# The order of TensorE's work in the softmax layer, and the routing of tokens inside the linear layer

## The reference

```python
att = where(causal, q @ k.T * SCALE, -inf)        # 16 heads of 16, 1024 tokens a batch
y = softmax(att) @ v @ W_proj + b_proj            # softmax layer
y = x @ weight.T + pooled(x) @ disha              # its second half, one matrix here
# linear layer: Q, K = elu(x @ W) + 1;  out = num / den with running sums over tokens
num = Q @ cumsum(K.T V);  den = max(Q . cumsum(K), 1e-6);  x + (num / den) @ Wo
x + gelu(layernorm(x) @ Wf1) @ Wf2
# mixture of experts: 8 experts, 2 per token, 1.05 capacity
probs = softmax(xf @ Wg);  topv, topi = top_k(probs, 2);  gates = topv / sum(topv)
pos = running count of earlier tokens (and choices) of the same expert
keep = pos < cap;  dest = where(keep, expert * cap + pos, none)
buf[dest] = xf;  y = expert(buf);  out = sum over both choices of gate * keep * y[dest]
```

## Time and profile before

| what | value |
|---|---|
| median of 3 runs | 4939.04 us (4929.02 to 4948.95) |
| the profiled execution | 4914.62 us, its span 4912.8 us |
| mean granted TensorE clock | 0.921 of full speed |
| PE busy | 4128.4 us (84%) |
| DVE busy | 2642.9 us (54%) |
| ACT busy | 1873.6 us (38%) |
| POOL busy | 968.0 us (20%) |
| softmax layer | about 150 to 1390 us |
| linear layer | about 1510 to 3658.8 us |
| routing | 3659.1 to 3861.0 us |
| experts, combine | to 4704 us, 4707 to 4913 us |

### The profile page before, as it was taken

The page is one execution under the profiler, slowest core; times in us unless marked ns, Lnnn a source line. Parts: engine busy times, 40 slices in busy tenths (PEclk is TensorE's granted clock), DMA queues, the critical chain, the costliest instruction groups (busy, mean ns, idle before and its releaser), DMA issues. The chain is left out here.

```text
span 4912.8 us, 74344 instructions
## 1 busy us (share of the span) xinstructions
PE 4128.4 (84%) x26008; PEld 3048.3 (62%) x26008; DVE 2642.9 (54%) x7485; ACT 1873.6 (38%) x2968; POOL 968.0 (20%) x1013
## 2 busy tenths in 40 slices
PE   5999999999947999999999999999960499999920
PEld 2344444444426777777777787777740398999920
DVE  4787788778716444444444554444440354454546
ACT  1566566656633333333333333333310233233300
POOL 3333343333222000000000000000007200000056
PEclk8999999989778999999999999999975699999965
DMA  4353335333311000000000000000003222121146
GB/s 70 67 89 71 58 67 97 71 58 59 63 42 46 14 14 14 14 14 12 3 14 14 14 14 14 14 14 14 9 26 117 76 64 81 58 64 58 46 129 158
DMA packets 191422, 238.30 MB, mean 49 GB/s; under 512 B 27372, under 2 KB 168651, under 8 KB 191040
## 3 DMA queue, kind: packets, MB, share of 16 engines
q1 hardware_dynamic: 152256, 180.19, 16.1%
q0 software_dynamic: 12288, 26.83, 2.2%
q10 hardware_dynamic: 26496, 26.22, 1.6%
HBM read 102.41 MB, written 86.11 MB: 38 GB/s over the span
## 5 line engine op out<-in xcount | busy, mean ns | idle before, releaser
L762 ACT ACTIVATE probs<-a_scores 128x1024 f32<-128x1024 f32 (+3 forms) x768 | 615.1, 811 | 376.2 <-PE a_scores L666 369.9
L923 DVE CUSTOM_DVE_ANT_0 a_scores<-a_scores,mask 128x384 f32<-128x384 f32 (+3 forms) x1024 | 481.3, 515 | 124.2 <-PE a_scores L652 117.1
L1677 DVE TENSOR_TENSOR l_a<-l_general,l_a 128x512 f32<-128x512 f32 x64 | 44.3, 692 | 736.8 <-PE l_general L1307 736.8
L235 POOL TENSOR_TENSOR l_ln_rstd<-l_ln_ve,minus_half 128x4 f32<-128x4 f32 x80 | 82.8, 1035 | 1670.0 <-DVE l_ln_ve L208 1670.0
L666 PEld LDWEIGHTS a_scores<-q_st,k_st 50*128 50x128 f32 x1536 | 151.2, 194 | 410.5 <-issue 279.8
L666 PE MATMUL a_scores<-q_st,k_st 50*128 50x512 f32 (+3 forms) x1536 | 354.6, 459 | 34.5 <-issue 25.6
L926 DVE TENSOR_REDUCE mx<-a_scores 128x2 f32<-128x1024 f32 x256 | 311.0, 1223 | 115.4 <-PE a_scores L652 114.3
L686 PE MATMUL a_out<-probs,v_aug 128*32 128x512 f32 (+3 forms) x3072 | 350.6, 531 | 2.8 <-POOL probs L855 2.7
L652 PE MATMUL a_scores<-k_st,q_st 48*128 48x512 f32 (+3 forms) x1536 | 309.9, 401 | 47.1 <-ACT probs L762 28.8
L2115 PE MATMUL e_out<-e_weights_hi,e_hT_lo 128*128 128x256 f32 x1088 | 304.1, 279 | 0.0
L2115 PE MATMUL e_out<-e_weights_lo,e_hT_hi 128*128 128x256 f32 x1088 | 304.1, 279 | 0.0
(11 more groups left out here) (239 smaller groups left out, 9564.5 us busy)
## 6 DMA issues: line engine op xcount, KB each, us to landing
q_st<-parts SPq DMA_DIRECT2D x192, 128.0 KB, 4.6
k_st<-parts SPq DMA_DIRECT2D x192, 128.0 KB, 6.7
expert_rows_scratch<-zero SPq DMA_DIRECT2D x8, 2176.0 KB, 12.7
e_weights<-in_L_ffn_W_dram SPq DMA_DIRECT2D x16, 1024.0 KB, 6.3
e_rows<-expert_rows_scratch SPq DMA_DIRECT2D x24, 384.0 KB, 3.3
expert_out_scratch<-e_y ACTq DMA_DIRECT2D x24, 384.0 KB, 2.5
x_in<-in_L_attn_x_dram SPq DMA_DIRECT2D x8, 1024.0 KB, 5.5
x_res<-in_L_attn_x_dram SPq DMA_DIRECT2D x8, 1024.0 KB, 5.5
```

What stands on the lines that cost most here:

```text
L762: nc.scalar.activation(probs[:, k % 3, 2 * pair:2 * pair + 2, 0:w], psum_r[:, R.slot(u), :, 0:w], ACT.Exp).then_inc(R.evacuated[R.slot(u)], 1)
L923: last = nc.vector.tensor_tensor_reduce(s, s, mask[:, HALF - w:HALF], 1.0, LEAST, ALU.add, ALU.max, out[:, h2, :])
```

## The change

Two things are changed.

In the softmax layer TensorE makes both scores and both maxima of a position first, and then the values of position `k-2` and the unit. The numbering of the ring's uses stays.

The function `routing` is gone. In the linear layer the logits of a group stay in a small tile; while the next group runs, VectorE makes the choice of both experts in twelve small steps in chunks 0 to 5, TensorE counts in chunk 8 with six bf16 products into the free end of the state update's PSUM bank, VectorE takes the counts up in that chunk and works out rows in chunks 9 to 11. GpSimd copies the norms into a tile `rows` (it lies in the memory of the high half of the next group's input) and scatters them with eight indirect transfers; VectorE waits for their landing before it makes that high half. For the last group all of it follows the last logits. In `combine` the gates are made from the kept gap of both logits, in five small instructions ahead of the first group. The stores and loads of `xf_scratch` are gone.

```diff
                         scores(b, RU, k, 0)
                         if more:
                             maxima(b + (k + LM) // NK, b, RU, k + LM, 0)
+                        scores(b, RU, k, 1)
+                        if more:
+                            maxima(b + (k + LM) // NK, b, RU, k + LM, 1)
                         if k > 1:
                             values(b, RU, k - 2)
                         elif with_tail:
                             values(b - 1, RU_TURN, NK - 2 + k)
-                        scores(b, RU, k, 1)
-                        if more:
-                            maxima(b + (k + LM) // NK, b, RU, k + LM, 1)
...
+                for e in range(E):
+                    nc.gpsimd.memset(index[:, e:e + 1], float(e - E)).then_inc(made, 1)
...
                     store(g - 1, 1 - s)
                     if not last:
-
+                        sp.wait_ge(xf_ready, g)
+                        sp.sem_inc(x2_read, 1)
                         sp.wait_ge(x3_stored, g * 16)
...
+                def counts(g):
+                    pe.wait_ge(picked_ready, g + 1)
+                    flat = both[:, :, :].rearrange("p t e -> p (t e)")
+                    at = lambda t: psum_u[:, COUNTS + t * E:COUNTS + (G4 + 1) * E]
+                    nc.tensor.matmul(psum_u[:, COUNTS:COUNTS + E], keep[:, :], flat[:, 0:E],
+                                     start=True, stop=True, skip_group_check=True)
+                    for d in range(1, G4 + 1):
+                        last = nc.tensor.matmul(at(d), ones[:, :], flat[:, 0:(G4 + 1 - d) * E],
+                                                start=(d == 1), stop=True, skip_group_check=True)
+                    return nc.tensor.matmul(psum_u[:, COUNTS + E:COUNTS + G4 * E], keep[:, :],
+                                            flat[:, E:G4 * E], start=False, stop=True,
+                                            skip_group_check=True)
...
                         UP.wait_free(pe, g, n)
+                        if n == COUNT_AT and not first:
+                            counts(g - 1)
...
-                        act.wait_ge(xf_stored, stored)
+                        act.wait_ge(rows_ready, stored)
...
+                def keep_rows(g, r, U):
+                    for u in range(U["QK"] + NQK - R, U["QK"] + NQK):
+                        G.wait_evacuated(pool, r, u)
+                    pool.wait_ge(xf_ready, g + 1)
+                    nc.gpsimd.tensor_tensor(
+                        rows[:, :, :], norm[:, :, :], one[:, :].rearrange(
+                            "p (j d) -> p j d", j=1).broadcast_to([P, G4, D]), ALU.mult
+                        ).then_inc(rows_ready, 1)
+
+                def scatter(g, src, copied=True):
+                    if copied:
+                        pool.wait_ge(rows_ready, g + 1)
+                    pool.wait_ge(to_ready, g + 1)
+                    pool.sem_inc(scatter_begun, 1)
+                    for j in range(G4):
+                        for k in range(2):
+                            nc.gpsimd.indirect_dma_start(
+                                out=rows_dram,
+                                out_offset=bass.IndirectOffsetOnAxis(ap=to[:, k, j:j + 1], axis=0),
+                                in_=src[:, j, :], in_offset=None,
+                                bounds_check=SLOTS - 1, oob_is_err=False).then_inc(scattered[k], 16)
+
                 def group(g, b, s, U, first, last_group):
                     if not first:
                         last_norms(g - 1, 1 - s)
+                        keep_rows(g - 1, g, U)
                     if not last_group:
                         for call in range(2):
                             ln1.power(pool, g + 1, call)
+                    if not first:
+                        scatter(g - 1, rows)
+                    if not last_group:
                         low(g + 1)
...
+                def choose(g, step):
+                    k, t = step // 6, t0[:, 0, :, :]
+                    src = left if k else lg
+                    if step == 0:
+                        route_chain.at = 0
+                    else:
+                        route_chain.wait(dve, g)
+                    if step % 6 == 0:
+                        ins = nc.vector.tensor_reduce(best[:, k, :], src[:, :, :], AX.X, ALU.max)
+                    elif step % 6 == 1:
+                        ins = nc.vector.tensor_tensor(t, src[:, :, :], over(best[:, k, :]), ALU.is_equal)
...
+                    else:
+                        nc.vector.tensor_tensor(gap[:, bass.ds(g * G4, G4)], best[:, 1, :],
+                                                best[:, 0, :], ALU.subtract)
+                        nc.vector.tensor_tensor(both[:, :, :], picked[:, 0, :, :], picked[:, 1, :, :],
+                                                ALU.add).then_inc(picked_ready, 1)
+                        return
+                    route_chain.mark(ins)
+
+                def take_counts(g):
...
+                def locate(g, step):
+
+                    route_chain.wait(dve, g)
...
+                    else:
+                        nc.vector.tensor_scalar(place[:, :, tiles], row[:, :, :], float(SLOTS), None,
+                                                ALU.add)
+                        nc.vector.tensor_scalar(to[:, :, :], row[:, :, :], float(SLOTS), None,
+                                                ALU.add).then_inc(to_ready, 1)
+                        return
...
+                CHOOSE = {n: (2 * n, 2 * n + 1) for n in range(6)}
+                LOCATE = {COUNT_AT + 1 + n: (2 * n, 2 * n + 1) for n in range(3)}
...
-                        den_chain.link(dve, g, nc.vector.tensor_scalar(den[:, 0, :], num[:, :, DH1],
-                                                                       EPS_DEN, None, ALU.max))
+                        den_chain.mark(nc.vector.tensor_scalar(den[:, 0, :], num[:, :, DH1],
+                                                               EPS_DEN, None, ALU.max))
+                        if not first and n in LOCATE:
+                            locate(g - 1, LOCATE[n][0])
+                        den_chain.wait(dve, g)
+                        if not first and n in CHOOSE:
+                            choose(g - 1, CHOOSE[n][0])
                         den_chain.link(dve, g, nc.vector.reciprocal(den[:, 1, :], den[:, 0, :]))
...
+                        if not first and n in CHOOSE:
+                            choose(g - 1, CHOOSE[n][1])
+                        if not first and n in LOCATE:
+                            locate(g - 1, LOCATE[n][1])
                         NUM.wait_evacuated(dve, g, n)
                         UP.wait_full(dve, g, n)
+                        if n == COUNT_AT and not first:
+                            take_counts(g - 1)
...
                     if not last_group:
+                        if not first:
+                            for k in range(2):
+                                dve.wait_ge(scattered[k], g * G4 * 16)
+                            dve.sem_inc(rows_gone, 1)
                         high(g, g + 1, U)
...
+                for step in range(12):
+                    choose(NGR - 1, step)
+                dve.wait_ge(counted, 1)
+                take_counts(NGR - 1)
                 for k in range(2):
+                    dve.wait_ge(scattered[k], (NGR - 1) * G4 * 16)
+                for step in range(6):
+                    locate(NGR - 1, step)
```

More of the change, by code:

```diff
@@ L1166, in linear_layer @@
         diff = scores[:, 0, :, :, :].rearrange("p c h q -> p c (h q)")
+        ones = sb("l_ones", [P, P], BF16)
+        index = sb("l_index", [P, E])
+        lg = sb("l_logits", [P, G4, E])
+        t0 = sb("l_route", [P, 2, G4, E])
+        left = t0[:, 1, :, :]
+        best = sb("l_best", [P, 2, G4])
+        which = sb("l_which", [P, 2, G4])
+        picked = sb("l_picked", [P, 2, G4, E], BF16)
+        both = sb("l_both", [P, G4, E], BF16)
+        base = sb("l_base", [P, E])
+        one = sb("l_one", [P, 1])
+        count = lg
+        row = sb("l_row", [P, 2, G4])
+        to = sb("l_to", [P, 2, G4], I32)
+        COUNTS = 320
         load = sem("l_weights_loaded")
@@ L1604, in _ @@
                 last_norms(NGR - 1, 1)
+                scatter(NGR - 1, norm, copied=False)
+                for k in range(2):
+                    pool.wait_ge(scattered[k], NGR * G4 * 16)
             @block.vector
```

255 lines of the change are left out of this document (92 added, 163 removed).

## The result

The changed kernel takes 5074.0 us (median of 4 runs, 5052.3 to 5101.6), against 4934.0 for the kernel before in the same measurements (4913.6 to 4949.0): ratio 1.029, interval 1.022 to 1.036. The forecast was 4930, its range 4855 to 5045.

What follows compares the result with a forecast made beforehand. TensorE was taken to bound the softmax and linear layers, GpSimd's 128 scatters the 202 us between linear layer and experts. Routing -157.5, softmax order +130 and clock +20 gave -7.5: 4930 us, range 4855 to 5045.

Steps and rivals of the forecast that it cites:

- Routing's tail: Between last logits and experts' first weight load: eight scatters instead of 128 save 173 us, bounds 165 to 180.
- the way from the last scatter to the load: End of routing, before the experts: taken as 12.73 us as before, perhaps up to 7 us less.
- The linear layer's steps: 22 small VectorE steps in each of 15 groups' chunk loops: +15 us in all, 8 to 38.
- The scatters beside the chunk loop: Linear layer: eight scatters a group delay the high half by 1.5 us against 8.3 us of slack, costing nothing.
- rival C: Linear layer: scatters slowed beside VectorE use up the slack, 14 us, up to 60 with copy uncovered; 4945 to 4990; chance 0.12.
- one slow gather of `combine`: Trace row the prediction called a scatter next to VectorE, 1.90 us in place of 0.97; used to price slowed scatters.
- The softmax stall: Softmax layer: second maxima wait uncovered for the exponential; net 18.2 us a batch, +130 us in all, floor 75, ceiling about 300.
- The slot and the ready time of 1.76 us: Softmax ring: second maxima reuse the first scores' slot, free once the exponential is done, 1.70 to 1.77 us after the start.
- the smaller of idle and values: Softmax positions: each grows by the smaller of TensorE's idle and the values' time; sum 21.1 us a batch.
- the last three positions: End of each softmax batch: left out of the sum, taken up by a 5.10 us wait for the last maxima's way through memory.
- The clock: Softmax layer: frequent short TensorE idles bring more half clock, +20 us (0 to 120).
- Rival B: Softmax layer: clock falls from one idle in each position, some +115 us, 5045; sign a clock below 0.85; chance 0.2.

Runs made afterwards that it cites:

- e3: Changed kernel with the old softmax order, scatters of the first 15 groups left out; 4777.9 us, ratio 0.967 to the kernel before.
- e2: Changed kernel with the softmax layer's old order restored, so only the routing is new; 4876.8 us, ratio 0.987 to the kernel before.
- e1: Kernel before with only the new softmax order; 5121.1 us, ratio 1.037 to the kernel before.
- e6: Changed kernel with the old softmax order, only each token's first choice scattered in the loop, four transfers a group; 4776.1 us, ratio 0.969.
- e7: Changed kernel with old softmax order, rows in the second norm's transposes, ScalarE waiting for landing, scatters still ahead of the low half; 4874.3 us, ratio 0.989.
- e4: Changed kernel with old softmax order, rows in the second norm's transposes, scatters issued behind the low half, ScalarE waiting for landing; 4788.7 us, ratio 0.967.
- e5: Changed kernel with old softmax order, the loop's eight scatters replaced by plain transfers of the same bytes on SyncE's queue; 4786.3 us, ratio 0.971.
- e9: Changed kernel with old softmax order, GpSimd waiting after each two scatters of the loop for their landing; 4785.9 us, ratio 0.969.
- e12: e4 plus nine never-read 512-column products on TensorE ahead of its wait at each softmax batch's turn; 4831.2 us, ratio 0.979 to the kernel before.

## Why the prediction was wrong, point by point

**Routing's tail**, forecast -173 (165 to 180), measured -182.4: right in kind. The choice steps took 2.7 us (forecast 2.5), the counts on TensorE 0.5 (1.5), the locating steps 1.4 (1.6), GpSimd's start 0.9 behind the last (1.1), eight scatters 1.29 apart. What was missized is the way from the last scatter to the load, 4028.2 - 4023.4 = 4.8 us and not 12.7; I had named up to 7 us there.

**The linear layer's steps**, forecast +15, measured +22.6 in e3, inside 8 to 38.

**The scatters beside the chunk loop**, forecast at nothing, with rival C at 14 to 60. They cost 97 us. This is the step that failed most. Two assumptions were wrong. I followed the scatters only to VectorE's wait for their landing, and nothing is lost there. And I priced their interference by one slow gather of `combine` on GpSimd itself (1.90 us; the prediction calls it a scatter), while the losers are the two engines that wait for TensorE. GpSimd's own intervals stayed at 1.28 us. The trace of before had no place where GpSimd's transfers ran beside waits on TensorE, so the bound could not be read from it, and "nothing" was no bound. VectorE's unnamed waits are 86.9 us in 15 groups, part of which it would have idled in any case. By e2 against e3 the 97 us are 71 of TensorE's idle and 26 of slower products; its clock, at 1.00 in the earlier trace rows, is 0.97 in the changed kernel. The Trainium skill's rule on the port pair that VectorE and GpSimd share ("SBUF — State Buffer", section "Who interferes with whom") does not describe it: GpSimd was not slowed, and ScalarE was held too.

**The softmax stall**, forecast 18.2 us a batch, measured 18.2 (29.7 - 11.5) in the changed kernel and 19.3 in e1. The slot and the ready time of 1.76 us were right; the rule "the smaller of idle and values" was not tested by itself. The waits for the exponential are 138.0 us in the 1200, where the prediction looked for some 200. That the last three positions hide in the turn was wrong in its reason, and the turn's idle shrank by only 0.5 us (5.10 to 4.6), yet the sum came out, to that extent by luck.

**The clock**, forecast +20 (0 to 120), measured: 85 us of longer busy time up to the linear layer (14.0 a batch, 56 in four batches), beside 140 of idle. The order alone made 46 of them (e1); some 20 came with the routing and the old order (e2), and the rest is not told apart. The prediction had no term for a clock that shifts without a change in the layer. That it was half or full clock was read rightly; which share was not. The row of one stall of 0.92 us followed by 0.51 spoke for it, three stalls that lowered nothing spoke against, and I let three rare stalls stand for 350 frequent ones. Rival B had the mechanism with +115 on top of the sum, 135 for the clock in all, which was too much; its time of 5045 fell short all the same, since it had nothing for the scatters. Its sign, a softmax clock below 0.85, just failed to show (0.86 in the softmax window of the earlier trace rows, 0.87 over four batches, 0.85 up to the linear layer). The rule of the Trainium skill, "TensorE: Matmul & The Clock Gate", section "A second HAM failure mode: psum-queue depth-cycling", foresaw it. Here the granted clock swings between its two levels, 0.87 on average over four batches against 0.96.

**The sum.** Two terms failed: the scatters, which had no price at all, and the clock, which had a quarter of it. The forecast was -7.5 on the profiled execution, measured +170.9: 97 from the scatters, 65 from the clock (85 for 20), 10 from the stall (140 for 130), 8 from the steps, 5 more in the linear layer and 3 behind it that no run names, less 9 from the tail: 179, against a miss of 178.4.

## What stays open

Why transfers of GpSimd hold back the takers of TensorE's results is not settled. Shown are: without the scatters it is gone (e3), four beside the loop don't cause it (e6), it is neither VectorE's wait for the landing nor the place of the rows in SBUF (e7), it goes when they run beside long products (e4), and it ends 2.4 us behind the last scatter's start, when the burst's packets are through. The same bytes in a shorter burst of SyncE don't cause it (e5). Whether it takes more than four scatters under way at once, or a fifth one beside the loop however slow they are, is open: e9 has neither. Paced scatters that begin early enough for all eight to stand beside the loop would tell. Whether TensorE's signals arrive late, or the waiting engines see them late, or fetch their next code late, no run tells apart. That ScalarE and VectorE are both held speaks against a single engine's code.

What decides where the clock's low stretches fall is open too, and so is the cause of the 5 us at each turn of the softmax layer's loop.

## What to carry to other kernels

Price an asynchronous transfer by everything that runs beside it, not only by who waits for it: the same eight scatters cost 97 us beside a loop of short handshakes, 6 us behind it, and about 2 when pacing left four beside the loop and put four behind it. And price a stall on TensorE twice: once as idle, once for the clock. Here 19.3 us more idle a batch, in pieces of 0.6 to 0.8, came with 9 us of slower work in e1, and 18.2 with 14 in the changed kernel. Filling about half of each piece with useless products took e1's ratio from 1.037 to 1.029: better than the idle, and still worse than the order that has none of it. The version to keep is e4 or e9, which can't be told apart: the routing part with late or paced scatters and the old softmax order: 3.3 and 3.1% faster than the kernel before.

## What the runs showed of the hardware that was not expected

- GpSimd's transfers in a burst of eight hold the takers of TensorE's results for up to 6.5 us; with bursts of four (e6) VectorE waited 1.6 us at most for a numerator.
- The same softmax code on the same data ran at 163.9 and at 170.6 us a batch in different kernels, with equal idle, and over four batches a clock of 0.96 and 0.92. So a difference of 20 us in this layer can come from an edit elsewhere.
- TensorE idles 5 us at each turn of the softmax layer's loop, also ahead of products that need none of the batch's data (4.78 us in e12), and some 0.5 us less when its positions stall (4.6 in the changed kernel). In the 12 us behind it the clock of the kernel before is 0.59.
- Products of no use behind such an idle bring the clock back (0.54, then 1.00 within the filler of e12), at their own cost in time.
